# Recommender head on one Trainium2 core: the odd batch tiles enter the weight stream 57 units behind the even ones instead of 43

## The chip, the cores and the metric

The kernel runs on one core of a Trainium2 chip. The metric is device time in microseconds of one launch, the median of several executions. All data is fp32 in HBM at the start and the scores are in HBM at the end.

## What is computed

For 1024 samples. `x` is [1024, 50, 300], `label_embedding` is [1024, 200, 300]. Cut to what matters:

```python
def _attn_pool(x, mask, w_a, b_a, w_b):
    score = exp((x @ w_a + b_a) @ w_b)
    score = where(mask == 0, PAD, score)
    p = softmax(score, axis=1)
    return einsum('bne,bn->be', x, p[..., 0])
mask = sign(sum(abs(x), axis=2))[..., None]
q1 = _attn_pool(x, mask, w1, b1, w2)
q2 = _attn_pool(x, mask, w3, b3, w4)
h = concatenate([q1, q2], axis=1) @ w5 + b5          # [1024, 300]
f6 = h @ w6 + b6
iu, ju = triu_indices(300, k=1)                       # 44850 pairs
g = (v @ v.T)[iu, ju]
f7 = (h[:, iu] * h[:, ju] * g) @ w7 + b7              # w7 is [44850, 300]
out8 = concatenate([f6, f7], axis=1) @ w8 + b8
return einsum('bu,bku->bk', out8, label_embedding)    # [1024, 200]
```

The cost lies in three places: f7 (44850 products per sample, and a matmul over them), the two dot products of each of the 50 (padded to 56) rows of x, and the dot products with the 200 label rows of each sample.

## The kernel before

**Work and tiles.** The samples are cut into 8 batch tiles of 128 (b = 0 to 7), and for x into 16 half tiles of 64. The 44850 pairs are laid out as 351 tiles of 128 pairs, grouped by a table of 91 *units* (`UNITS`, `unit_table()`), most of them of four tiles. A unit names its left operand (A, B, C or a rotated copy such as A64, all parts of h transposed) and one of 25 buffers of rotated right operands. The first 57 units use the eight A buffers (seven units each, eight in the first), then come the B buffers (units 57 to 81), then six units of the rest, then three units ("own", units 88 to 90) whose two operands are both gathered in small pieces. The end of the table with these three is called a turn in what follows. VectorE multiplies left and right into `cring` (`products`, L917 for two batch tiles at once, L905 once per tile where only one is live; four slots), and TensorE multiplies them with the unit's part of w7 into the batch tile's accumulator (`unit`, L600, 128 x 300 fp32, which the trace shows as two MATMULs).

**The counter q.** Every engine walks through the same steps q, from START = -34 to STOP. Step q of 0 to POS - 1 does unit q of the stream, which is entry q mod 91 of the table. w7 is streamed over and over, in blocks of two units (1200 KB, `w7_load`, L729, from ScalarE's queue, three slots). Batch tile b takes part from BEGIN[b] to END[b] = BEGIN[b] + 91. Even tiles begin at 0, 91, 182, 273, odd ones SHIFT units later. While two are live, one block of w7 serves both. So SHIFT units at the head and SHIFT units at the end have one tile (*one-tile units*), all others two (*two-tile units*). In two-tile units ScalarE multiplies w7 by g (`w7_scale`, L738); in one-tile units VectorE folds g into its products. POS is the last END, 407 before.

**x and its dots.** Half tile s is read by the steps DOTS[s] = (first, past the last). In each of them VectorE makes the share of 56 dot rows (`score_row`, L819), ScalarE the sums of absolute values (`absolute`, L663). Maxima, softmax weights, pooling on TensorE (L549), turning and the product with w5 (`mix`, L563) follow at fixed distances (`LATE`): MIX is 12 steps behind the last dot step, and writes the left operands of tile b, in the buffers that tile b - 4 had.

**Labels.** Behind END[b] the tile's f7 is closed and out8 made. From LATER = 11 steps behind END[b], the 200 label rows of tile b are worked off, 150 KB each, loaded by fives (a *chunk* of 750 KB, `l_load`, L391, from SP's queue): VectorE makes one dot per row (`label_row`, L935). LABELS_BY says how many rows are done by the end of a step. For tile b they are spread over the steps up to END[b+1] + LATER, where a step that also has x dots counts one and another counts two. For tile 6, only EARLY_ROWS of its rows are done before POS. All other rows of tiles 6 and 7 come after POS, five a step, without any unit beside them: TAIL_CHUNKS chunks. Four in five of these are *shared*: VectorE makes the product of the chunk (L931), ScalarE the five row sums (`sums`, L747).

**Loads of h.** h is written to HBM (`hrows`) and read back in rotated form by SP's queue (`s_load`, L426 for the buffers, L433 to L446 for the three "own" units in many small pieces), for each live tile, three slots ahead. They stand in the same queue as x and labels, in the order of q.

**What the change and the steps of the prediction touch:** SHIFT (L140) and through it BEGIN, END, POS and BOTH; DOTS (L166); EARLY_ROWS (L205) and LABELS_BY; `products`, `unit`, `w7_scale`, `label_row`, `sums`.

Of the kernel before, what the change touches and what calls it, by code (L numbers as in the profile page):

```python
# [32 lines left out]
def unit_table():  # L33

    units, buf = [], 0
    for k in range(NA):
        first = 1 if k == 0 else 0
        units.append(("A", buf, first, QUAD - first))
        units.append(("B", buf, 0, QUAD))
        if k == 0:  # L40
            units.append(("A32", buf, 0, 1))
        units.append(("A64", buf, first, QUAD - first))
        for left in ("B32", "B64", "B96", "C"):
            units.append((left, buf, 0, QUAD))
        buf += 1
    for k in range(NB):
        first = 1 if k == 0 else 0
        units.append(("B", buf, first, QUAD - first))
        if k == 0:
            units.append(("B32", buf, 0, 1))  # L50
        units.append(("B64", buf, first, QUAD - first))
        units.append(("C", buf, 0, QUAD))
        buf += 1
    for k in range(ND):
        units.append(("A", buf, 0, QUAD))
        units.append(("B", buf, 0, QUAD))
        buf += 1
    for n in CUSTOM:
        units.append(("own", buf, 0, n))
        buf += 2  # L60
    return units, buf
# [37 lines left out]
UNITS, BUFS = unit_table()  # L99
# [7 lines left out]
def rec_kernel(nc, x, label, w13, w24, w5, w6t, w8, bcols, b8, w7p, vleft, vright, out):  # L107
# [29 lines left out]

    SHIFT = next(k for k, u in enumerate(UNITS) if u[1] == 6)  # L140
    BEGIN = [NU * (b // 2) + SHIFT * (b % 2) for b in range(NBT)]
    END = [p + NU for p in BEGIN]
    POS = END[-1]
    BOTH = END[-2] - SHIFT

# [4 lines left out]
    def live_at(n):  # L150
# [13 lines left out]


    DOTS = [(-34, -27), (-27, -20), (-20, -6), (-6, 6), (6, 24), (24, 43), (43, 54), (54, 65), (65, 77), (77, 89),  # L166
            (100, 114), (123, 137), (146, 160), (169, 183), (192, 206), (215, 229)]
    START = DOTS[0][0]
    ROWS = [(t // T, t % T, hd) for t in range(TT) for hd in range(2)]

# [31 lines left out]


    LATER = 11
    EARLY_ROWS = 65  # L205
    LABELS_BY = {START - 1: 0}
    for q in range(START, POS):
        done = 0
        for b in range(NBT - 1):
            steps = range(END[b] + LATER, END[b + 1] + LATER if b < NBT - 2 else POS)  # L210
            share = [1 if any(a <= k < z for a, z in DOTS) else 2 for k in steps]
            rows = K if b < NBT - 2 else EARLY_ROWS
            done += rows * sum(w for k, w in zip(steps, share) if k <= q) // sum(share)
# [30 lines left out]
    with ctx:  # L244
# [280 lines left out]
        def _(pe):  # L525
# [57 lines left out]
            def unit(p):  # L583
# [5 lines left out]
                pe.wait_ge(c_ready, p + 1)  # L589
                if SHIFT <= p < SHIFT + BOTH:  # L590
                    pe.wait_ge(w7_ready, p - SHIFT + 1)
                else:
# [50 lines left out]
        def _(act):  # L643
# [80 lines left out]
            def w7_load(n):  # L724
                k = BLOCKS[n][1]
                a, z = UNIT_TILE[k * WUNITS] * E, UNIT_TILE[min((k + 1) * WUNITS, NU)] * E
                if n >= WSLOTS:
                    act.wait_ge(c_used, LAST[n - WSLOTS] + 1)
                act.dma_start(wring[:, n % WSLOTS, 0:z - a], w7p[:, a:z]).then_inc(w7_in[n % WSLOTS], 16)  # L729

            def w7_scale(p):
                n, u = BLOCK_OF[p], p % NU
                first = UNIT_TILE[FROM[n] % NU]
                if p == max(FROM[n], SHIFT):
                    act.wait_ge(w7_in[n % WSLOTS], 16 * (n // WSLOTS + 1))
                for t in range(UNIT_TILE[u], UNIT_TILE[u + 1]):
                    w = wring[:, n % WSLOTS, (t - first) * E:(t - first + 1) * E]
                    ins = nc.scalar.activation(w, w, ACT.Copy, scale=gcol[:, t:t + 1])  # L738
                ins.then_inc(w7_ready, 1)
# [13 lines left out]
            for q in range(START, STOP):  # L753
# [7 lines left out]
                if 0 <= q < POS:  # L761
                    if q in FROM and FROM.index(q) + 2 < len(BLOCKS):
                        w7_load(FROM.index(q) + 2)
                    if SHIFT <= q + AHEAD < SHIFT + BOTH:
                        w7_scale(q + AHEAD)
# [241 lines left out]
```

## Time and profile before

| | us |
|---|---|
| median of 3 runs | 1860.07 |
| lowest, highest | 1859.95, 1860.88 |
| the profiled execution | 1859.29 |
| its span, first to last instruction | 1857.5 |
| TensorE busy | 1615.5 (87%) |
| VectorE busy | 1479.9 (80%) |
| ScalarE busy | 919.1 (49%) |
| moved by DMA | 617 MB, mean 332 GB/s |
| mean granted TensorE clock | 0.952 |

The engines overlap, so the busy times don't add up. A share is a mean over the head (x alone, then one-tile units), the long middle with two tiles, the one-tile units at the end and the labels behind them; each has its own limit, and what 14 units more or less are worth there is read from the stretch itself.

### The profile page before, as it was taken

The numbers are of one execution on the slowest core, as the hardware profiler recorded it, in microseconds if no ns is written. First come the engines' busy times: TensorE is split into PE (matmuls) and PEld (weight loads), VectorE is DVE, ScalarE is ACT, GpSimd is POOL, SyncE is SP. The second block draws the span as 40 slices with busy tenths as digits, with TensorE's granted clock in tenths as the row PEclk, the third lists the DMA queues.
The fourth block names the chain that finished last, engine by engine and source line by source line (L and its number), as shares of the span: only waits on it lengthen the run. The fifth ranks groups of instructions, "written<-read, shape, count | busy, mean of one in ns | idle before, by whom it ended". The sixth has DMA issues, their size and how long they took to land.

```text
span 1857.5 us, 25035 instructions
## 1 busy us (share of the span) xinstructions
PE 1615.5 (87%) x7142; PEld 1165.1 (63%) x7142; DVE 1479.9 (80%) x5516; ACT 919.1 (49%) x2844; POOL 33.4 (2%) x62
## 2 busy tenths in 40 slices
PE   0569999999999999997999999999999999998300
PEld 0236677776777767774777777767777777666200
DVE  8898986863699989967899976758777677498996
ACT  4433376654564636463465634434444444200698
POOL 0000000000000000000000000000000000000000
PEclk9889999999999999998999999999999999999655
DMA  7669867767789898998989999999999899899895
GB/s 279 237 256 352 344 245 260 264 222 278 263 301 420 324 401 335 389 334 308 381 300 407 352 394 386 364 294 403 355 342 342 305 385 354 272 420 421 338 417 244
DMA packets 139215, 617.00 MB, mean 332 GB/s; under 512 B 16432, under 2 KB 43693, under 8 KB 106181
## 3 DMA queue, kind: packets, MB, share of 16 engines
q1 hardware_dynamic: 105157, 368.23, 52.8%
q10 hardware_dynamic: 31744, 244.16, 34.0%
q0 software_dynamic: 2176, 3.01, 0.5%
q8 instruction: 57, 0.93, 0.2%
q14 instruction: 81, 0.66, 0.1%
HBM read 611.55 MB, written 3.79 MB: 331 GB/s over the span
## 4 chain that ended last, share of the span: by engine, by line
PE 72%; DMA 7%; ACT 7%; DVE 7%; SPq 4%; issue 2%; ACTq 0%; POOL 0%; DVEq 0%; POOLq 0%
PE bank L600 64%; ACT stream L747 6%; DMA wring<-in_w7p 5%; DVE junk L819 3%; PE bank L549 3%; SPq L438 3%; PE bank L563 2%; DMA sring<-hrows 2%; DVE stream L935 1%; PE bank L612 1%; PE bank L610 1%; DVE cring L917 1%; DVE cring L905 1%; ACT absjunk L663 1%; SPq L444 0%
## 5 line engine op out<-in xcount | busy, mean ns | idle before, releaser
L600 PE MATMUL bank<-wring,cring 128*128 128x300 f32 (+1 forms) x5616 | 1448.0, 419 | 52.8 <-DVE cring L917 19.6
L600 PEld LDWEIGHTS bank<-wring,cring 128*128 128x128 f32 (+1 forms) x5616 | 1064.1, 191 | 420.8 <-DVE cring L905 30.4
L738 ACT ACTIVATE wring<-wring,gcol 128x300 f32<-128x300 f32 x1237 | 565.1, 533 | 608.8 <-PE bank L600 340.3
L935 DVE SCALAR_TENSOR_TENSOR stream<-stream,out 128x300 f32<-128x300 f32 x1335 | 546.4, 466 | 0.9 <-DMA stream<-in_label 0.2
L917 DVE TENSOR_TENSOR cring<-lefts,sring 128x1024 f32<-128x1024 f32 (+2 forms) x309 | 368.3, 1193 | 205.1 <-PE bank L600 202.6
L819 DVE SCALAR_TENSOR_TENSOR junk<-stream,ubc 128x300 bf16<-128x300 f32 x896 | 364.2, 466 | 4.3 <-DMA stream<-in_x 4.2
L663 ACT ACTIVATE absjunk<-stream 128x300 bf16<-128x300 f32 x448 | 196.3, 440 | 50.3 <-PE bank L600 48.6
L747 ACT ACTIVATE stream<-stream 128x300 f32<-128x300 f32 x265 | 115.5, 441 | 0.1
L549 PE MATMUL bank<-stream,wts 128*32 128x300 f32 x896 | 66.6, 453 | 55.8 <-DVE small L861 55.8
L935 DVE DVE_READ_ACCUMULATOR stream<-stream,out 128x1 f32 x1335 | 109.9, 82 | 0.0
L905 DVE SCALAR_TENSOR_TENSOR cring<-lefts,gcol,sring 128x128 f32<-128x128 f32 x334 | 95.2, 348 | 16.8 <-PE bank L600 15.7
L931 DVE TENSOR_TENSOR stream<-stream,out 128x1500 f32<-128x1500 f32 x53 | 89.6, 1717 | 3.5 <-DMA stream<-in_label 1.8
L549 PEld LDWEIGHTS bank<-stream,wts 128*32 128x32 f32 x896 | 29.8, 118 | 90.8 <-issue 66.3
L663 ACT ACTIVATION_READ_ACCUMULATOR absjunk<-stream 128x1 f32 x448 | 84.6, 189 | 0.0
L819 DVE DVE_READ_ACCUMULATOR junk<-stream,ubc 128x1 f32 x896 | 74.0, 83 | 0.0
L917 DVE TENSOR_TENSOR cring<-sring 128x1024 f32<-128x1024 f32 (+1 forms) x12 | 11.5, 956 | 72.4 <-DMA sring<-hrows 49.1
L652 ACT ACTIVATE flat<-bank 128x300 f32<-128x300 f32 x8 | 3.2, 405 | 105.6 <-PE bank L600 105.6
L747 ACT ACTIVATION_READ_ACCUMULATOR stream<-stream 128x1 f32 x265 | 50.5, 190 | 0.0
L563 PE MATMUL bank<-poolT,w5sb 128*128 128x128 f32 (+3 forms) x288 | 48.2, 297 | 1.0 <-ACT poolT L652 0.8
L563 PEld LDWEIGHTS bank<-poolT,w5sb 128*128 128x128 f32 (+3 forms) x288 | 35.2, 164 | 14.4 <-issue 4.5
L838 DVE TENSOR_SCALAR masked<-absum 128x28 f32<-128x28 f32 x16 | 2.9, 178 | 38.6 <-ACT small L669 38.6
L655 ACT ACTIVATE lefts<-bank,bcol 128x128 f32<-128x128 f32 x16 | 5.9, 366 | 43.6 <-PE bank L563 42.7
(62 smaller groups left out, 247.7 us busy)
## 6 DMA issues: line engine op xcount, KB each, us to landing
stream<-in_label SPq DMA_DIRECT2D x320, 750.0 KB, 8.2
wring<-in_w7p ACTq DMA_DIRECT2D x184, 1200.0 KB, 8.4
stream<-in_x SPq DMA_DIRECT2D x64, 1050.0 KB, 12.6
sring<-hrows SPq DMA_DIRECT2D x152, 256.0 KB
wring<-in_w7p ACTq DMA_DIRECT2D x9, 1050.0 KB, 8.6
wring<-in_w7p ACTq DMA_DIRECT2D x9, 600.0 KB, 7.5
lefts<-hrows SPq DMA_DIRECT2D x48, 64.0 KB, 2.6
sring<-hrows SPq DMA_DIRECT2D x32, 88.0 KB
```

Source lines behind the costliest of these rows:

```text
L438: sp.dma_start(tiles[r0:r1, j0:j0 + ni, :], src).then_inc(s, 16)
L549: pe.matmul(dst[j * M:(j + 1) * M, 0:E], wts[:, j * T + t].rearrange("p h b -> p (h b)"), xring[:, X_SLOT[s * PARTS + j], t, :], start=(t ...
L563: mm = pe.matmul(dst[0:n, 0:P], w5sb[0:nk, q, o:o + n], poolT[0:nk, q % NCH, q // NCH, :], start=(q == 0), stop=(q == 2 * NCH - 1))
L600: mm = pe.matmul(acc[b % 4][:, 0:E], cring[0:rows, p % CSLOTS, b % 2, j0 + j, :], w, start=(p == BEGIN[b] and j == 0), stop=(p == END[b] - ...
L663: nc.scalar.activation(absjunk[:, k % 2, :], xring[:, X_SLOT[n], r % T, :], ACT.Abs, accum_out=absum[:, s % 3, r:r + 1]).then_inc(abs_done, 1)
L738: ins = nc.scalar.activation(w, w, ACT.Copy, scale=gcol[:, t:t + 1])
L747: ins = nc.scalar.activation(row, row, ACT.Copy, accum_out=score[:, m % 2, q0 + k:q0 + k + 1])
L819: ins = nc.vector.scalar_tensor_tensor(out=junk[:, k % 2, r % 2, :], in0=xring[:, X_SLOT[n], t, :], scalar=1.0, in1=ubc[:, hd, 0:E], op0=A ...
L905: ins = nc.vector.scalar_tensor_tensor(out=cring[0:rows, p % CSLOTS, b % 2, j, :], in0=one, scalar=gcol[0:rows, t:t + 1], in1=sring[0:rows ...
L917: nc.vector.tensor_tensor(cut(cring, p % CSLOTS), in0, cut(sring, nb % SSLOTS), ALU.mult).then_inc(c_ready, 1)
L931: nc.vector.tensor_tensor(rows, rows, out8[:, m % 4, :].unsqueeze(1).to_broadcast([P, LR, E]), ALU.mult).then_inc(l_product, 1)
L935: ins = nc.vector.scalar_tensor_tensor(out=row_in, in0=row_in, scalar=1.0, in1=out8[:, m % 4, :], op0=ALU.mult, op1=ALU.mult, accum_out=sc ...
```

## The change

SHIFT is now the first unit of buffer 8 (the first B buffer), 57, where it was the first unit of buffer 6, 43. Worked out from the table: odd tiles begin at 57, 148, 239, 330 (before 43, 134, 225, 316); POS is 421 for 407; the units with two tiles are 57 to 363, 307 for 321; w7 is read in 213 blocks for 206. The last six half tiles' dots are moved: the first of them by 3 steps, the others by 6. EARLY_ROWS is 95 for 65, so TAIL_CHUNKS is 61 for 67 and the shared chunks are 48 for 53. The intervals over which a tile's 200 label rows are spread, END[b] + 11 to END[b+1] + 11, are 57 and 34 steps long in turn, where they were 43 and 48.

```diff
-    SHIFT = next(k for k, u in enumerate(UNITS) if u[1] == 6)
+    SHIFT = next(k for k, u in enumerate(UNITS) if u[1] == 8)
...
     DOTS = [(-34, -27), (-27, -20), (-20, -6), (-6, 6), (6, 24), (24, 43), (43, 54), (54, 65), (65, 77), (77, 89),
-            (100, 114), (123, 137), (146, 160), (169, 183), (192, 206), (215, 229)]
+            (103, 117), (129, 143), (152, 166), (175, 189), (198, 212), (221, 235)]
...
-    EARLY_ROWS = 65
+    EARLY_ROWS = 95
```

What it does to VectorE's order at three places. Names: `cring` holds the products for TensorE, `junk` takes the x dots, `stream` is the ring of x and label rows.

VectorE at unit 43 and behind it, before:

```order
L905 SCALAR_TENSOR_TENSOR cring<-lefts,gcol,sring 128x128 x4
L819 SCALAR_TENSOR_TENSOR junk,small<-stream,ubc 128x300 x3
L917 TENSOR_TENSOR cring<-lefts,sring 128x1024
L819 SCALAR_TENSOR_TENSOR junk,small<-stream,ubc 128x300 x5
L838 TENSOR_SCALAR masked<-absum 128x28
```

The same place now:

```order
L905 SCALAR_TENSOR_TENSOR cring<-lefts,gcol,sring 128x128 x4
L819 SCALAR_TENSOR_TENSOR junk,small<-stream,ubc 128x300 x3
L905 SCALAR_TENSOR_TENSOR cring<-lefts,gcol,sring 128x128 x4
L819 SCALAR_TENSOR_TENSOR junk,small<-stream,ubc 128x300 x5
L838 TENSOR_SCALAR masked<-absum 128x28
```

The dot rows stay where they were; the product beside them is that of one tile in four instructions, for units 43 to 56.

VectorE at units 178 and 179 (the last before the "own" units, and the first of these), before:

```order
L917 TENSOR_TENSOR cring<-lefts,sring 128x1024
L819 SCALAR_TENSOR_TENSOR junk,small<-stream,ubc 128x300 x4
L935 SCALAR_TENSOR_TENSOR stream,score<-stream,out 128x300 x3
L917 TENSOR_TENSOR cring<-sring 128x1024
L819 SCALAR_TENSOR_TENSOR junk,small<-stream,ubc 128x300 x4
```

Now:

```order
L917 TENSOR_TENSOR cring<-lefts,sring 128x1024
L819 SCALAR_TENSOR_TENSOR junk,small<-stream,ubc 128x300 x4
L935 SCALAR_TENSOR_TENSOR stream,score<-stream,out 128x300 x4
L917 TENSOR_TENSOR cring<-sring 128x1024
L819 SCALAR_TENSOR_TENSOR junk,small<-stream,ubc 128x300 x4
```

There are four to five label rows a step beside four dot rows, for three before; in the steps of this interval without dots there are eight or nine.

VectorE at the end of the units (L931 is the first shared chunk), before:

```order
L905 SCALAR_TENSOR_TENSOR cring<-lefts,gcol,sring 128x128 x4
L935 SCALAR_TENSOR_TENSOR stream,score<-stream,out 128x300 x2
L905 SCALAR_TENSOR_TENSOR cring<-lefts,gcol,sring 128x128 x4
L935 SCALAR_TENSOR_TENSOR stream,score<-stream,out 128x300 x3
L931 TENSOR_TENSOR stream<-stream,out 128x1500
```

Now:

```order
L905 SCALAR_TENSOR_TENSOR cring<-lefts,gcol,sring 128x128 x4
L935 SCALAR_TENSOR_TENSOR stream,score<-stream,out 128x300 x2
L905 SCALAR_TENSOR_TENSOR cring<-lefts,gcol,sring 128x128 x4
L935 SCALAR_TENSOR_TENSOR stream,score<-stream,out 128x300 x8
L931 TENSOR_TENSOR stream<-stream,out 128x1500 x4
```

The one-tile units with some two label rows each run for 14 units more, and the labels behind them begin with one chunk that isn't shared.

## Rows read from the trace of the kernel before

**Rows 1.** the page's slices, TensorE, busy tenths of 40 equal slices
```profile
PE   0569999999999999997999999999999999998300
```

**Rows 2.** stretches: start:end us, length, then each engine's busy us (instructions), PEclk, DMA share, GB/s
```profile
105.80:172.20 66.40, 54.29 (x269) 36.95 (x270) 60.44 (x284) 20.10 (x84) 3.52 (x6) 1.00 0.81 322
172.20:220.30 48.10, 43.39 (x220) 30.58 (x219) 45.41 (x210) 14.68 (x62) 0.00 (x0) 1.00 0.93 363
220.30:280.70 60.40, 60.40 (x296) 44.32 (x295) 50.42 (x198) 41.95 (x135) 0.00 (x0) 1.00 0.66 245
280.70:482.80 202.10, 199.07 (x999) 142.67 (x998) 123.08 (x435) 117.61 (x361) 7.04 (x12) 0.99 0.72 262
482.80:733.70 250.90, 250.90 (x1117) 184.97 (x1116) 228.39 (x900) 140.77 (x405) 7.59 (x13) 1.00 0.90 343
733.70:896.10 162.40, 148.52 (x662) 106.25 (x661) 130.98 (x518) 76.48 (x213) 0.00 (x0) 0.95 0.94 349
896.10:1147.50 251.40, 251.25 (x1120) 185.19 (x1119) 215.48 (x832) 132.74 (x365) 8.15 (x14) 1.00 0.95 368
1147.50:1285.00 137.50, 134.82 (x531) 99.53 (x530) 94.36 (x319) 58.87 (x133) 0.58 (x1) 1.00 0.96 352
1285.00:1515.30 230.30, 230.30 (x911) 171.94 (x910) 169.21 (x574) 103.00 (x231) 0.58 (x2) 1.00 0.94 344
1515.30:1622.20 106.90, 103.25 (x403) 77.04 (x402) 64.79 (x214) 40.81 (x91) 0.00 (x0) 0.98 0.94 324
1622.20:1650.50 28.30, 25.18 (x94) 16.45 (x94) 28.30 (x134) 1.71 (x5) 0.00 (x0) 1.00 1.01 412
1650.50:1680.80 30.30, 27.14 (x103) 18.58 (x102) 27.86 (x123) 0.00 (x0) 0.54 (x1) 1.00 1.01 419
1680.80:1720.20 39.40, 35.24 (x136) 24.82 (x134) 31.85 (x133) 0.00 (x0) 0.00 (x0) 1.00 1.01 422
1720.20:1857.50 137.30, 16.02 (x43) 8.51 (x41) 117.75 (x199) 117.15 (x535) 1.08 (x2) 0.54 0.82 332
```

**Rows 3.** the same columns for instructions on cring alone (PE, PEld, DVE), units 284 to 340
```profile
1285.00:1515.30 230.30, 225.70 (x894) 169.35 (x893) 68.54 (x58) 1.00 0.94 344
```

**Rows 4.** waits, 1640 to 1730 us: waiter <- awaited, total us, times, longest
```profile
PE bank L600 <- DMA wring<-in_w7p: 8.6, 13, 1.7
```

**Rows 5.** DMA issues, 1640 to 1730 us: count, KB each, median us to landing
```profile
wring<-in_w7p ACTq DMA_DIRECT2D x17, 1200.0 KB, 9.8
stream<-in_label SPq DMA_DIRECT2D x17, 750.0 KB, 27.4
```

**Rows 6.** groups by line, ScalarE from 1728 us: busy us, mean ns, idle before
```profile
L747 ACT ACTIVATE stream<-stream 128x300 f32<-128x300 f32 x265 | 115.5, 441 | 0.1
```

**Rows 7.** timeline of VectorE, 218 to 222 us: start us, us, instruction
```profile
218.12 1.14 DVE L905 SCALAR_TENSOR_TENSOR cring<-lefts,gcol,sring 128x128 f32<-128x128 f32 x4
219.18 0.46 DVE L819 SCALAR_TENSOR_TENSOR junk<-stream,ubc 128x300 bf16<-128x300 f32 x1
...
220.35 1.22 DVE L917 TENSOR_TENSOR cring<-lefts,sring 128x1024 f32<-128x1024 f32 x1
221.49 0.47 DVE L819 SCALAR_TENSOR_TENSOR junk<-stream,ubc 128x300 bf16<-128x300 f32 x1
```

**Rows 8.** waits, 790 to 880 us, the turn of units 179 to 181
```profile
DVE cring L917 <- issue: 12.1, 2, 10.1
...
DVE cring L917 <- DMA sring<-hrows: 9.4, 1, 9.4
```

**Rows 9.** stretches as in rows 2: two turns, and units 375 to 406
```profile
1220.00:1250.00 30.00, 28.52 (x114) 21.17 (x113) 12.17 (x40) 10.36 (x24) 0.00 (x0) 1.00 0.91 288
1590.00:1620.00 30.00, 26.34 (x99) 19.42 (x98) 9.52 (x33) 7.74 (x17) 0.00 (x0) 0.94 0.86 253
1650.50:1720.20 69.70, 62.39 (x237) 43.40 (x235) 59.71 (x255) 0.00 (x0) 0.54 (x1) 1.00 1.01 421
```

**Rows 10.** waits of the loading queue SP, 1150 to 1290 us
```profile
SPq L391 <- DVE stream L935: 58.7, 19, 4.1
```

## The prediction

> **What bounds the kernel now.** I read four views, in this order, and tied each to the counter that orders the program, the unit number (0 to 406). The slices of the page come first [rows 1]: TensorE stands at nine tenths nearly all the way from the fifth slice to the thirty-seventh. The last two have no TensorE work and belong to the labels. To see where a unit lies in time, the stretches [rows 2] are cut at unit starts, which the products themselves show: in the stretches of product work alone [rows 3], 2 x 57 batch-tile units give 58 VectorE instructions and 894 matmul instructions. That stretch (units 284 to 340) took 230.3 us, 4.04 us a unit, with TensorE busy throughout and its clock at full speed. A unit of two batch tiles is 16 matmul instructions of 225.70/894 = 0.2525 us, which is those 4.04 us; a unit of one tile is 8 of them, **2.02 us at TensorE's pace**.
>
> Three kinds of time follow. With two tiles live (units 43 to 363, 220.3 to 1622.2 us) TensorE sets the pace: it is busy 60.4 of 60.4, 199.1 of 202.1, 230.3 of 230.3 us, and loses only in the stretches around the turns of the unit table (units 88 to 90, 179 to 181, ...), 13.9 us in units 159 to 192. With one tile live a unit does not run at 2.02 us: units 24 to 42 took 48.1 us, 2.53 each, with VectorE busy 45.4 us of it; units 390 to 406 took 39.4 us, **2.32 each**, with the transfers at 422 GB/s [rows 2]. There TensorE waits 13 times, shortly, for the w7 block [rows 4]; a block takes 9.8 us to land and a label chunk 27.4 us [rows 5]. After the last unit the labels have 137.3 us to themselves, ScalarE busy for 117.2 of it [rows 2], nearly all in row sums: 265 of them, 115.5 us [rows 6].
>
> By the starts of VectorE's instructions [rows 7], the four products of a one-tile unit take 1.06 us (218.12 to 219.18), three dot rows 1.17, so 0.39 each (to 220.35), the product of a two-tile unit 1.14 (to 221.49). Label rows have the same shape and I give them the same 0.39.
>
> **The change, part by part.** Total matmul work is the same. Fourteen units that had two tiles become twenty-eight with one: 14 at the head (43 to 56) and 14 behind the old end (407 to 420). The w7 stream is read for 421 units in place of 407, seven more blocks of 1200 KB [rows 5], 8.6 MB. ScalarE scales w7 for 14 units less; it is busy 103.0 us of 230.3, so that hides and is worth nothing.
>
> Head, units 43 to 101. It took 60.4 + 202.1 = 262.5 us. It loses 14 x 4 matmuls of two instructions, 112 x 0.2525 = 28.3 us. But the x dots of tile 3 have not moved, so VectorE keeps its 50.4 busy us, less 14 x 0.08. By the ratio of busy time to span in the two one-tile stretches before it (60.4 of 66.4, 45.4 of 48.1) 49.3 us of work take 52 to 54 us; I take 53. TensorE's own part there is 60.4 + about 11 of work that it carried over (its lag of up to four units) - 28.3 = 43 us, so 10 us of idle time come in. 262.5 - 28.3 + 10 = 244.2: **-18.3 us** (-21 to -14).
>
> The label rate. Tile b's 200 rows are spread evenly from END[b]+11 to END[b+1]+11. These intervals were 43 and 48 units long and are now 57 and 34. In the three short ones the rate is 5.9 rows a unit for 4.2. In the long ones (units 102 to 158, 193 to 249, 284 to 340) TensorE was busy 250.9 of 250.9, 251.3 of 251.4 and 230.3 of 230.3 us already, and fewer rows bring nothing: **0**.
>
> Units 159 to 192. Label rows go from 156 to 200, and because the dots were moved later, the dot rows from 64 to 84. 64 rows x 0.39 = 25.1 us on a VectorE that was busy 131.0 of 162.4, so 156.1. It also stood idle for the small loads of the turn, 9.4 and 12.1 us [rows 8], which more rows do not shorten, since they are in its own order behind the products: 156.1 + 21.5 = 177.6, **+15.2** (0 if the idle time takes them up, +25 if none does).
>
> Units 250 to 283. 58 more label rows of 150 KB are 8.9 MB; 137.5 us at 352 GB/s were 48.4 MB, now 57.3. In the 30 us of the turn the queues moved only 288 GB/s [rows 9], 8.6 MB. The other 48.7 MB at the 421 GB/s held in units 375 to 406 take 115.7 us; 145.7 us in all, **+8.2**. TensorE's 134.8 and VectorE's 94.4 + 22.7 = 117.1 lie under it. Units 341 to 374: 106.9 at 324 and 28.3 at 412 GB/s are 46.3 MB, plus 8.9 is 55.2; the turn took 7.6 MB in 30 us (253 GB/s), the rest 113.1 us: 143.1 for 135.2, **+7.9**. Ends for each: 0, and +26 if the bytes move at the stretch's old mean (57.3/0.352 = 163; 55.2/0.342 = 161).
>
> Here the Trainium skill speaks against 421 GB/s: its page "DMA: Bandwidth & Descriptors", section "Where 436 GB/s comes from", says that for HBM to SBUF the HBM side binds, at about 358 GB/s. The trace disagrees, since 421 were held for 69.7 us [rows 9]; by the rule the two stretches would take 160 and 154 us and the sum be 26 us higher.
>
> Units 375 to 406: 66 label rows for 65, the same 31 or 32 units: 0. Units 407 to 420: fourteen at the 2.32 us of the seventeen before them, **+32.5**; ends 28.3 (TensorE's 2.02) and 35.4 (the 2.53 of units 24 to 42).
>
> The label tail. 30 more rows of tile 6 are done beside the units (95 for 65), so 61 chunks stay for 67, and 48 shared chunks for 53. Five times five row sums of 115.5/265 = 0.436 us: **-10.9**. By the mean of a chunk (137.3/67) it would be -12.3; if VectorE or a load took over, down to -8. ScalarE stays the bound: 61 chunks are 47 MB, 111 us at 421, with up to 13 in the ring before the tail.
>
> Sum: -18.3 + 15.2 + 8.2 + 7.9 + 32.5 - 10.9 = +34.6. The profiled execution took 1859.29 (span 1857.5), 0.8 below the median of the three runs, 1860.07: **1894 us**, slower by 1.8%.
>
> **Rivals.** *The dense stretches cost nothing.* VectorE's idle time and the rings take up the burst of labels: -18.3 + 32.5 - 10.9 = +3.3, 1863 us. For it: VectorE had 31 idle us in units 159 to 192 and 43 in 250 to 283. Against: two thirds of the first is the wait at a turn. Chance 0.10, on both sides of the 0.2% (3.7 us) that a measurement of this kernel can tell from no change.
>
> *One-tile units at TensorE's pace,* the one on the other side. If dots and w7 loads keep up with 2.02 us, the head loses all of its 28.3 us, the tail adds 28.3 and the labels give back 10.9: 1848 us, if the dense stretches cost nothing. With the head at my 53 us it decides from 2.09 us a unit at the tail downwards: 14 x 2.09 = 29.2 = 18.3 + 10.9. For it: units 375 to 389 took 30.3 us, 2.02 each [rows 2]. Against: the seventeen behind them did not, at the same row rate, and at the head VectorE alone has 49.3 us of work where TensorE's pace asks for 43. Chance 0.04.
>
> *The queues don't hold 421 GB/s in a mixed stretch.* Units 250 to 283 and 341 to 374 carry w7, labels and many small loads, and reached 352 and 342 GB/s without being short of requests. If these are their limits, those two cost 25 and 26 us in place of 8 and 8, and the tail units 35.4: 1894 + 17 + 18 + 3 = 1932 us. For it: the transfers' busy share was 0.96 already at 352 GB/s [rows 2]. Against: the queue that issues the label loads waited 58.7 us, 19 times, for VectorE to free a slot [rows 10], so the rate was what was asked for. The 358 of the skill's page named above would mean this case. Chance 0.18.
>
> **How the numbers follow.** Forecast 0.68, for 1894 us; its own bounds (the dense stretches between 10 and 50 together, the tail 28.3 to 35.4) reach from 1868 to 1915. I leave out the fast rival, most of the one at 1863 and what of the slow one lies beyond its price: **1866 to 1934**. Faster by over 0.2%: 0.04. Within: 0.05, from the case at 1863. Slower: 0.91.
>
> **What would show it right or wrong.** In the changed profile: the first two-tile product (L917) should stand at 273 us for 220.3; units 43 to 56 should show VectorE over 0.9 busy and TensorE near 0.8. Unit 102 should begin near 464.5 for 482.8. Units 159 to 192 should take about 178 us with VectorE at 156. The stretches 250 to 283 and 341 to 374 should take some 145 us at over 380 GB/s, with waits for label or w7 loads on the path. From the last two-tile unit to the end of units should be 57 one-tile units in 138 us for 43 in 98. ScalarE's row sums should be 240, and the part behind the last unit 126 us. The forecast is wrong if the head takes over 60 us (VectorE's rows are slower beside one-tile products), if unit 364 begins within 10 us of where the head leaves it (no cost of dense labels), or if the last fourteen units run at 2.1 us.

## The result, and the profile after

The changed kernel takes **1917.72 us**, the median of 4 runs (1914.53 to 1922.06), against 1860.01 for the kernel before on the same chip (4 runs, 1859.52 to 1860.88): ratio 1.0311, 95% interval 1.0289 to 1.0333. It is slower by 57.7 us. The forecast was 1894 us, slower, with a range of 1866 to 1934. The profiled execution is the longest of the four, 1922.06 us with a span of 1920.3, so the trace below explains 62.8 us.

The stretches of the changed kernel, cut at the same unit starts as [rows 2] and with the same columns (length, busy us of PE, PEld, DVE, ACT, POOL, PEclk, DMA share, GB/s). In order: units 43 to 56, 57 to 101, 102 to 158, 159 to 192, 193 to 249, 250 to 283, 284 to 340, 341 to 363, 364 to 374, 375 to 406, 407 to 420, and the rest:

```profile
219.40:269.00 49.60, 44.74 (x234) 30.25 (x233) 48.86 (x240) 21.30 (x90) 2.37 (x5) 1.00 0.81 300
269.00:461.00 192.00, 188.22 (x948) 134.84 (x947) 119.67 (x419) 114.02 (x351) 4.65 (x8) 0.99 0.74 275
461.00:723.80 262.80, 257.16 (x1117) 187.75 (x1116) 206.89 (x780) 136.34 (x381) 7.13 (x13) 0.97 0.82 305
723.80:908.00 184.20, 157.88 (x693) 111.92 (x691) 154.43 (x640) 88.14 (x251) 0.48 (x1) 0.94 0.91 335
908.00:1145.30 237.30, 237.30 (x1053) 175.03 (x1054) 195.35 (x728) 124.40 (x346) 4.00 (x7) 1.00 0.87 338
1145.30:1312.30 167.00, 149.42 (x566) 107.39 (x565) 117.09 (x434) 60.55 (x136) 4.24 (x8) 0.93 0.96 363
1312.30:1542.60 230.30, 230.30 (x911) 171.91 (x910) 146.56 (x457) 103.55 (x232) 0.97 (x2) 1.00 0.86 312
1542.60:1656.80 114.20, 104.14 (x401) 77.39 (x399) 80.17 (x294) 40.09 (x89) 0.00 (x0) 0.94 0.96 348
1656.80:1692.50 35.70, 29.15 (x100) 18.27 (x99) 35.70 (x172) 1.71 (x5) 0.00 (x0) 0.95 1.01 413
1692.50:1765.30 72.80, 64.63 (x246) 45.56 (x246) 60.54 (x263) 0.00 (x0) 0.54 (x1) 1.00 1.01 420
1765.30:1794.20 28.90, 25.67 (x98) 17.98 (x98) 25.40 (x109) 0.00 (x0) 0.00 (x0) 1.00 1.01 421
1794.20:1920.30 126.10, 16.19 (x45) 8.53 (x43) 107.02 (x184) 106.27 (x485) 1.08 (x2) 0.55 0.81 329
```

Against [rows 2] the difference, stretch by stretch:

| units | before | forecast of the change | after | change |
|---|---|---|---|---|
| 43 to 101 | 262.5 | -18.3 | 241.6 | -20.9 |
| 102 to 158 | 250.9 | 0 | 262.8 | +11.9 |
| 159 to 192 | 162.4 | +15.2 | 184.2 | +21.8 |
| 193 to 249 | 251.4 | 0 | 237.3 | -14.1 |
| 250 to 283 | 137.5 | +8.2 | 167.0 | **+29.5** |
| 284 to 340 | 230.3 | 0 | 230.3 | 0.0 |
| 341 to 374 | 135.2 | +7.9 | 149.9 | +14.7 |
| 375 to 406 | 69.7 | 0 | 72.8 | +3.1 |
| 407 to 420 | none | +32.5 | 28.9 | +28.9 |
| behind the units | 137.3 | -10.9 | 126.1 | -11.2 |

Head, the fourteen units behind the old end, and the label tail came out within 4 us of their terms. The largest part that was not forecast lies in units 250 to 283, around the turn at units 271 and 272. Ten microseconds at a time, there:

```profile
1230.00:1240.00 10.00, 10.00 (x42) 7.50 (x41) 1.69 (x10) 4.69 (x11) 0.00 (x0) 1.00 1.02 357
1240.00:1250.00 10.00, 6.21 (x25) 4.42 (x24) 3.32 (x12) 3.04 (x7) 0.00 (x0) 1.00 1.02 281
1250.00:1260.00 10.00, 2.27 (x9) 1.35 (x8) 0.26 (x2) 1.42 (x3) 0.00 (x0) 0.81 0.75 204
1260.00:1270.00 10.00, 5.78 (x12) 3.94 (x13) 4.72 (x19) 0.00 (x0) 0.00 (x0) 0.50 0.43 132
1270.00:1280.00 10.00, 9.79 (x38) 6.51 (x37) 10.00 (x44) 2.77 (x7) 0.00 (x0) 1.00 0.94 349
1280.00:1290.00 10.00, 8.38 (x28) 5.14 (x27) 10.00 (x40) 6.39 (x16) 0.00 (x0) 0.85 1.01 426
1290.00:1300.00 10.00, 10.00 (x25) 5.78 (x25) 7.78 (x32) 3.34 (x8) 0.00 (x0) 0.64 1.01 412
1300.00:1310.00 10.00, 10.00 (x41) 7.55 (x40) 8.85 (x30) 3.60 (x8) 0.00 (x0) 1.00 1.02 415
```

TensorE is busy 6.21, then 2.27 of 10 us, and the clock that it is granted falls to 0.81 and 0.50, which is 1.2 of 2.4 GHz; it comes back (1.00) and falls once more (0.85, then 0.64). In 1290 to 1300 us TensorE is busy all ten microseconds and gets through 25 matmul instructions, where it does 41 at full clock in the next ten. Before, the clock stayed at 1.00 over the whole of this stretch [rows 2]. While TensorE waits the transfers move only 281, 204 and 132 GB/s. In the first of these rows the DMA engines were nevertheless busy all the time (share 1.02, with which they moved 426 GB/s in 1280 to 1290 us); only in the next two, at 0.75 and 0.43, had they time to spare. What VectorE waited for, first after, then before:

```profile
DVE cring L917 <- issue: 15.0, 2, 12.7
DVE cring L917 <- DMA sring<-hrows: 15.0, 1, 15.0
```

```profile
DVE cring L917 <- DMA sring<-hrows: 10.4, 1, 10.4
DVE cring L917 <- issue: 4.7, 1, 4.7
```

30.0 us for the turn's gathers, where it was 15.1. (The "issue" waits stand before products of the same gathered operands, whose smallest DMAs the view gives no landing for, so I count them with the gathers.) From the product of unit 269 to that of unit 272 VectorE took 40.7 us, for 25.1 before; the same measure, three products of a turn, is used for the other kernels below. And the queue that issues them, with start and length:

```profile
1239.60 1.31 SPq L391 DMA_DIRECT2D stream<-in_label  x2
1241.07 9.76 SPq L438 DMA_DIRECT2D sring<-hrows  x6
1250.88 0.57 SPq L391 DMA_DIRECT2D stream<-in_label  x1
1251.62 4.54 SPq L438 DMA_DIRECT2D sring<-hrows  x6
```

Label chunks (L391) stand between the gathers (L438), and six gathers then take 9.76 us merely to be issued.

Units 102 to 158, forecast at zero, are a second such part, +11.9 us. TensorE did 1117 instructions there before and after, but now stood idle for 5.6 us of it, and its clock of 0.91 from 650.9 us on made its work 6.3 us longer:

```profile
650.90:723.80 72.90, 67.26 (x303) 46.07 (x302) 47.48 (x183) 27.98 (x77) 3.62 (x7) 0.91 0.82 317
```

```profile
690.70 1.36 PE L608 MATMUL bank<-brow,ones 1*128 1x300 f32 x2 [4.20 <-ACT poolT L652]
```

L608 begins out8 of tile 1, and stood behind ScalarE's copy of the turned pooled sums of half tile 11 (`poolT`). In the changed kernel both fall in step 151; before, they fell in steps 137 and 145. All five kernels of this document with SHIFT at 57 took 262.2 to 262.8 us in these units, with a wait of 4.2 to 4.8 us at this instruction and a mean clock of 0.97; all nine with 43, f1 with the moved dots among them, took 250.8 to 252.0 without that wait. So the shift of the tiles brings it; that the meeting in one step is the reason is argued from the trace and not shown, since no run separates the two in the changed kernel.

### The profile page after: what moved, and what is told of

The parts are those of the page before. It is cut to its first block, busy times and chain, and to the rows that moved or that the text cites. A ratio compares the mean times of both kernels' runs of the same rounds, so it can differ in the third digit from the quotient of the medians.

```text
span 1920.3 us, 25109 instructions
## 1 busy us (share of the span) xinstructions
PE 1638.1 (85%) x7142; PEld 1171.6 (61%) x7142; DVE 1495.1 (78%) x5659; ACT 884.3 (46%) x2738; POOL 33.2 (2%) x62
## 4 chain that ended last, share of the span: by engine, by line
PE 63%; DVE 14%; DMA 8%; ACT 7%; SPq 5%; issue 3%; ACTq 0%; POOL 0%; DVEq 0%; POOLq 0%
PE bank L600 55%; DMA wring<-in_w7p 5%; ACT stream L747 5%; DVE junk L819 5%; DVE stream L935 4%; SPq L438 3%; PE bank L563 2%; PE bank L549 2%; DMA sring<-hrows 2%; DVE cring L917 2%; DVE cring L905 2%; PE bank L612 1%; PE bank L610 1%; SPq L433 1%; ACT absjunk L663 1%
## 5 line engine op out<-in xcount | busy, mean ns | idle before, releaser
L600 PE MATMUL bank<-wring,cring 128*128 128x300 f32 x5616 | 1463.4, 421 | 98.3 <-DVE cring L917 52.2
L600 PEld LDWEIGHTS bank<-wring,cring 128*128 128x128 f32 x5616 | 1067.8, 192 | 478.9 <-DVE cring L917 61.8
L738 ACT ACTIVATE wring<-wring,gcol 128x300 f32<-128x300 f32 x1181 | 538.6, 532 | 620.2 <-PE bank L600 358.1
L935 DVE SCALAR_TENSOR_TENSOR stream<-stream,out 128x300 f32<-128x300 f32 x1360 | 556.7, 465 | 1.2 <-DMA stream<-in_label 0.7
L917 DVE TENSOR_TENSOR cring<-lefts,sring 128x1024 f32<-128x1024 f32 (+2 forms) x295 | 351.3, 1192 | 230.3 <-PE bank L600 227.1
L905 DVE SCALAR_TENSOR_TENSOR cring<-lefts,gcol,sring 128x128 f32<-128x128 f32 x446 | 126.6, 344 | 22.0 <-PE bank L600 14.8
L747 ACT ACTIVATE stream<-stream 128x300 f32<-128x300 f32 x240 | 104.6, 452 | 0.1
L917 DVE TENSOR_TENSOR cring<-sring 128x1024 f32<-128x1024 f32 (+1 forms) x12 | 11.5, 956 | 95.7 <-issue 59.8
L549 PEld LDWEIGHTS bank<-stream,wts 128*32 128x32 f32 x896 | 29.8, 118 | 90.1 <-issue 65.6
L931 DVE TENSOR_TENSOR stream<-stream,out 128x1500 f32<-128x1500 f32 x48 | 80.9, 1716 | 1.7 <-DMA stream<-in_label 0.2
L563 PE MATMUL bank<-poolT,w5sb 128*128 128x128 f32 (+3 forms) x288 | 48.1, 297 | 0.8 <-ACT poolT L652 0.8
L563 PEld LDWEIGHTS bank<-poolT,w5sb 128*128 128x128 f32 (+3 forms) x288 | 35.2, 165 | 14.2 <-issue 4.5
```

What stands on the lines that cost most here:

```text
L549: pe.matmul(dst[j * M:(j + 1) * M, 0:E], wts[:, j * T + t].rearrange("p h b -> p (h b)"), xring[:, X_SLOT[s * PARTS + j], t, :], start=(t ...
L563: mm = pe.matmul(dst[0:n, 0:P], w5sb[0:nk, q, o:o + n], poolT[0:nk, q % NCH, q // NCH, :], start=(q == 0), stop=(q == 2 * NCH - 1))
L600: mm = pe.matmul(acc[b % 4][:, 0:E], cring[0:rows, p % CSLOTS, b % 2, j0 + j, :], w, start=(p == BEGIN[b] and j == 0), stop=(p == END[b] - ...
L747: ins = nc.scalar.activation(row, row, ACT.Copy, accum_out=score[:, m % 2, q0 + k:q0 + k + 1])
L905: ins = nc.vector.scalar_tensor_tensor(out=cring[0:rows, p % CSLOTS, b % 2, j, :], in0=one, scalar=gcol[0:rows, t:t + 1], in1=sring[0:rows ...
L917: nc.vector.tensor_tensor(cut(cring, p % CSLOTS), in0, cut(sring, nb % SSLOTS), ALU.mult).then_inc(c_ready, 1)
```

## The experiments

**Theory A**: the label rate is what costs. The intervals of 57 and 34 steps in place of 43 and 48 make bursts of 5.9 rows a unit, all three of them over a turn. More label chunks are then freed, and so asked for, just where the gathers go through the same queue, and the gathers come late. **Rivals**: the offset of the tiles, or the later dots, with which TensorE's side work falls elsewhere (B); or the one-tile units themselves, by their queues or their own pace (E). Three sets of four kernels; in these the kernel before ran at 1863.63, 1860.98 and 1860.35 us (its single runs between 1852.88 and 1869.01), so differences under some 4 us are not told apart by medians.

**e1, the bursts alone, on the kernel before.** Used as `range(EDGES[b], EDGES[b + 1])` in the loop that fills LABELS_BY:

```diff
+    EDGES = (102, 159, 193, 250, 284, 341, 375, POS)
```

> The kernel before (odd tiles at 43, its own dots and EARLY_ROWS) with the label rows of the changed kernel's intervals: 200 rows between steps 102, 159, 193, 250, 284, 341 and 375. Theory A (the bursts of labels at 5.9 rows a unit cost the time, above all at the turns): units 102 to 374 take 50 to 64 us longer than before, as in the changed kernel, so 1910 to 1924 us. Rival B (the shifted tiles or the moved dots cost it): within 8 us of 1860. Rival C (more bytes than the queues carry, a matter of both): half, about 1885.

Measured 1903.05 us against 1863.63, ratio 1.0203 (1.0164 to 1.0243). Units 159 to 192, 193 to 249, 250 to 283 and 341 to 374:

```profile
736.80:914.90 178.10, 157.52 (x687) 112.78 (x686) 146.97 (x603) 79.41 (x220) 0.60 (x1) 0.93 0.95 357
914.90:1159.60 244.70, 244.70 (x1094) 180.28 (x1093) 194.47 (x717) 130.39 (x361) 8.04 (x14) 1.00 0.87 328
1159.60:1318.50 158.90, 141.54 (x539) 103.06 (x538) 116.65 (x435) 59.70 (x135) 0.07 (x1) 0.96 0.95 364
1546.80:1695.50 148.70, 134.65 (x491) 95.84 (x489) 115.75 (x461) 41.86 (x95) 0.00 (x0) 0.92 0.98 366
```

Units 102 to 374 took 1209.5 us for 1167.7, 41.8 more; the changed kernel took 1231.5, 63.8 more. So the bursts alone, with every tile, dot and one-tile unit where it was, bring two thirds of what was added to these stretches in the changed kernel. Of the other 22 us, 12.0 lie in units 102 to 158, which took 250.8 us here. The time lies below theory A's band (1910 to 1924), above rival C's 1885 and far above rival B's 8 us: A holds for most, not for all.

**e2, the changed kernel with the bursts of tiles 1 to 4 evened out.**

```diff
+    EDGES = (102, 159, 204, 250, 295, 341, 375, POS)
```

> The changed kernel with the label rows of tiles 1 to 4 spread evenly (intervals from 159 on: 45, 46, 45, 46 steps, 4.4 rows a unit); the last short interval, 341 to 375, stays. Theory A: units 159 to 192 fall from 184 to about 163 us, 250 to 283 from 167 to about 138, units 193 to 249 rise from 237 to about 250: 1880 to 1886 us. Rival B (shifted tiles, moved dots): 1912 to 1922.

1900.75 us (ratio to before 1.0191, 1.0156 to 1.0227), 17 less than the changed kernel (20.6, if each is held against the kernel before of its own set) and 15 short of theory A. Units 159 to 192 fell to 169.7 and 250 to 283 to 152.9, two thirds and half of the way back. An even rate of 4.4 rows does not restore the turns.

**e3, even, and no label rows at the turns.**

```diff
-            share = [1 if any(a <= k < z for a, z in DOTS) else 2 for k in steps]
+            share = [0 if k % NU >= 82 else 1 if any(a <= k < z for a, z in DOTS) else 2 for k in steps]
```

> As the even one, and no label rows in the nine steps up to and with each turn (q mod 91 of 82 to 90), the others of the interval somewhat denser. Theory A with its mechanism (a chunk of labels that is freed in the turn is loaded ahead of the turn's small loads in the same queue, and these come late): the waits at the turns shrink, another 10 to 20 us less than the even one, 1862 to 1872. Rival D (the small loads are slow by themselves, the labels only a matter of VectorE's and the queues' total): no less than the even one, 1880 to 1890.

1877.56 us (1.0083, 1.0050 to 1.0116), another 23 less, though 6 above theory A's band. Units 159 to 192 took 160.7 and 250 to 283 took 141.9; from unit 269 to unit 272 it was 23.3 us for e2's 32.8. The total number of rows and bytes is that of e2; only nine steps of each 91 are spared. Rival D, which had no less than the even kernel's time, is out.

**e4, the same on the kernel before**, which turns the reason into a gain:

```diff
-            share = [1 if any(a <= k < z for a, z in DOTS) else 2 for k in steps]
+            share = [0 if k % NU >= 82 else 1 if any(a <= k < z for a, z in DOTS) else 2 for k in steps]
```

> The kernel before with no label rows in the nine steps of each turn. TensorE lost 13.9 us in units 159 to 192, 2.7 in 250 to 283 and 3.7 in 341 to 363. Theory A with its mechanism: most of it comes back, 1843 to 1852 us. Rival D: 1858 to 1865, the waits at the turns as before.

**1841.42 us** (1841.40 to 1843.47), ratio 0.9882 (0.9849 to 0.9915): faster than both kernels, by 22 us against the median of before in its set, and a little more than theory A had expected. Units 159 to 192, 250 to 283 and 341 to 363:

```profile
731.60:887.70 156.10, 147.40 (x660) 105.63 (x659) 127.18 (x505) 74.34 (x207) 0.00 (x0) 0.97 0.92 347
1138.70:1274.50 135.80, 134.78 (x531) 99.53 (x530) 89.39 (x292) 57.66 (x130) 0.17 (x1) 1.00 0.92 352
1504.80:1599.60 94.80, 94.80 (x377) 71.36 (x376) 55.57 (x168) 40.57 (x91) 0.00 (x0) 1.00 0.88 335
```

The last, the third turn, took 94.8 us for 106.9, with TensorE busy in all of it. The span is 17.9 us shorter than that of before: -6.3, -1.7 and -12.1 in these three stretches, +4.7 in units 364 to 374, and small amounts elsewhere. The last two belong together, since TensorE does part of the third turn's work behind unit 364 now: units 341 to 374 took 127.8 us for 135.2, 7.4 less. The expectation had added up 20.3 us of lost TensorE time; the sum came near, but not by its parts: the turn of units 179 to 181, the first with label rows, was to give 13.9 us and gave 6.3. From unit 269 to 272 and from 360 to 363 VectorE took 16.7 us each, for 25.1 and 28.3 before.

**f1, only the dots moved, on the kernel before.**

```diff
-            (100, 114), (123, 137), (146, 160), (169, 183), (192, 206), (215, 229)]
+            (103, 117), (129, 143), (152, 166), (175, 189), (198, 212), (221, 235)]
```

> The kernel before with only the dots moved as in the change (the last six half tiles 3 and 6 steps later). Theory A (bursts of labels and the turns): the dots are of no account, 1856 to 1868 us. Rival B2 (the moved dots, which now begin 7 steps before the turn of units 179 to 181, cost it): units 159 to 192 at least 5 us longer than the 162.4 of before, and 1870 or more.

1862.58 us (1.0011, 0.9992 to 1.0030): no difference. Inside, the trace has units 159 to 192 in 166.4 us for 162.4 (rival B2 asked for 5 more), 193 to 249 in 241.7 for 251.4 and 250 to 283 in 150.0 for 137.5. The pooling and mixing of the last half tiles fall some steps later. 33 of the mixing's matmul instructions (L563), which had stood in units 193 to 249, come behind the start of unit 250, here and in the changed kernel: some 5.5 us, since 36 of them took 6.00 us there. The rest of the 12.5 us is 3.6 us more idle time of TensorE and a clock of 0.98. So of the 29.5 us in 250 to 283 some 5.5 are a shift and not a loss, with their counterpart in 193 to 249, which the forecast had at zero.

**f2, the changed kernel with EARLY_ROWS at 65.**

```diff
-    EARLY_ROWS = 95
+    EARLY_ROWS = 65
```

> The changed kernel with EARLY_ROWS back at 65: 30 label rows (4.6 MB) go from beside the last one-tile units to the label tail, which gets 10 to 11 us longer. Theory A with the queues as the bound of the one-tile units (421 GB/s): the 4.6 MB less make units 375 to 420 some 11 us shorter, 102 to 91, and the whole is the same, 1914 to 1922 us. Rival E (these units run at their own pace of w7 latency and TensorE): they stay at 102 us, and the whole is 1926 to 1930.

1920.59 us (1.0329, 1.0284 to 1.0374), not to be told from the changed kernel's 1.0311. Units 375 to 420, and the rest:

```profile
1682.30:1782.30 100.00, 90.09 (x343) 63.73 (x343) 76.44 (x313) 0.00 (x0) 0.54 (x1) 1.00 1.00 407
1782.30:1918.60 136.30, 16.12 (x44) 8.78 (x42) 117.31 (x197) 117.16 (x535) 1.08 (x2) 0.54 0.79 319
```

Thirty rows less made the 46 units 1.7 us shorter (100.0 for 101.7), while the tail grew by the expected 10.2 us. So these units were not bound by the sum of the bytes, as theory A had it: between 1.4 and 2.1 label rows each they take some 2.2 us whatever the labels do. Rival E had this right, but its 1926 to 1930 us for the whole did not come. The whole doesn't show the 8 us that follow, because the stretches ahead were some 10 us shorter in this execution, for no reason of the edit; the total decides nothing here, the stretch does.

**f3, even to the end, and turns free.**

```diff
+    EDGES = (102, 159, 204, 250, 295, 341, 386, POS)
```

> The changed kernel with all label intervals from tile 1 on even (the last from 341 to 386) and the turns free of label rows: nothing of the bursts is left. Theory A: units 341 to 374 fall from 151.7 to about 135, units 375 to 420 rise by the few rows that come there, 1862 to 1870 us. What stands then against the turn-free kernel before (1841) is the cost of the fourteen pairs of one-tile units themselves, +20 to +28; by the sum of head, tail and labels in the prediction it was +3. Rival: 1875 or more.

1881.92 us (1.0119, 1.0072 to 1.0166): no better than e3. Units 341 to 374 gave 22.7 us back (129.0 for e3's 151.7), and units 375 to 420 took nearly all of it. First f3, then e3:

```profile
1635.70:1761.90 126.20, 101.72 (x362) 69.34 (x361) 109.03 (x495) 0.00 (x0) 0.54 (x1) 0.95 1.01 420
```

```profile
1644.30:1749.90 105.60, 93.27 (x342) 65.72 (x343) 87.71 (x371) 0.00 (x0) 0.54 (x1) 0.97 1.01 419
```

By the schedule, 157 label rows stand beside these units in f3 and 95 in e3: 62 rows for 20.6 us, 0.33 us each, with the queues at 420 GB/s. Beyond about two rows a unit, a label row beside a one-tile unit costs about what it costs in the tail (f2: 10.2 us for thirty, 0.34 each). The expected 1862 to 1870 fell with that.

**f4, label rows kept, their loads moved behind the turn's gathers, to step 88.**

```diff
         free = L_END[L_BEFORE[n]] if L_BEFORE[n] is not None else X_WIDE_DONE if n < NARROW else X_DONE
+        if 82 <= free % NU < 88:
+            free += 88 - free % NU
```

> The kernel before with the label rows in their places, but every load of a label chunk that falls in steps 82 to 87 of a turn issued at step 88, behind the turn's gathers. Theory A's mechanism in its strict form (the labels' bytes stand ahead of the gathers in the same queue): most of the gain of the turn-free kernel, 1843 to 1852 us. Rival F (it is VectorE's rows in the turn, or the bytes of w7 on the other queue): 1858 to 1868 us.

1862.26 us (1.0007, 0.9985 to 1.0028): no gain, and by its number in rival F's band. (The profiled execution is the longest of nine, 1872.37 us.) But the waits moved with the loads, for which rival F gives no reason. (Lines stand two further down in this kernel and the next: L919 is L917, L393 is L391, L440 is L438, L446 is L444.) VectorE's products of units 179, 180 and 181 (start, length, idle time before), and the queue:

```profile
833.83 1.23 DVE L919 TENSOR_TENSOR cring<-sring 128x1024 f32<-128x1024 f32 x1 [3.43 <-issue]
...
839.75 1.23 DVE L919 TENSOR_TENSOR cring<-sring 128x1024 f32<-128x1024 f32 x1 [1.95 <-issue]
...
856.33 0.42 DVE L919 TENSOR_TENSOR cring<-sring 50x256 f32<-50x256 f32 x1 [12.61 <-issue]
```

```profile
841.00 1.78 SPq L393 DMA_DIRECT2D stream<-in_label  x4
842.95 1.97 SPq L446 DMA_DIRECT2D sring<-hrows  x4
```

The first two products, which had come 13.4 and 14.0 us behind the one before them, now came after 7.4 and 5.9; the third, whose gathers (L446) were still to be issued when four label chunks went out at step 88, came after 16.6 in place of 6.0. It was the same at the two later turns, 18.3 and 18.4 us ahead of the third product.

**g1, the same, but behind all gathers, for the wide ring.**

```diff
         free = L_END[L_BEFORE[n]] if L_BEFORE[n] is not None else X_WIDE_DONE if n < NARROW else X_DONE
+        if n >= L_WIDE and free % NU >= 82:
+            free += NU - free % NU
```

> The kernel before with its label rows in place; for the chunks of the wide ring (thirteen slots, from tile 3 on) a load that falls in steps 82 to 90 of a turn is issued in the first step behind it, behind all of the turn's gathers. In the earlier deferral (to step 88) four chunks stood in the midst of the gathers, and the wait moved to the last of them. Theory A's mechanism (bytes ahead of the gathers in their own queue): the two late turns (units 271 and 272, 362 and 363) take some 7 us each as in the turn-free kernel, in place of 13 and 8, 17 and 6; 250 to 283 falls by 3 to 6, 341 to 363 by 8 to 12, the first turn stays: 1843 to 1852 us. Rival F: 1858 or more.

1862.50 us (1.0011, 0.9984 to 1.0038): again no gain, and in rival F's band. At the two later turns the waits nevertheless went as theory A has it. From unit 269 to 272 VectorE took 16.8 us for 25.1, from 360 to 363 16.5 for 28.3, as little as in e4, while its label rows and the w7 loads stayed in their steps; its busy time in units 341 to 363 is the 64.79 us of before. So it is the loads of labels that delay the gathers, and rival F is out. The queue at the second turn, with the last twelve of fifteen gathers issued in 6.43 us (all fifteen in 10.66), where the changed kernel needed 9.76 for six and 4.54 for the next six:

```profile
1224.48 6.43 SPq L440 DMA_DIRECT2D sring<-hrows  x12
1231.07 1.28 SPq L446 DMA_DIRECT2D sring<-hrows  x4
```

and units 341 to 363, with the third turn, then units 375 to 406:

```profile
1514.00:1609.20 95.20, 95.20 (x378) 71.63 (x377) 64.79 (x214) 40.96 (x92) 0.00 (x0) 1.00 0.85 304
...
1640.40:1724.30 83.90, 66.66 (x246) 46.48 (x246) 59.17 (x255) 0.00 (x0) 0.54 (x1) 0.96 1.01 421
```

95.2 us for 106.9, as in e4 (126.4 for 135.2 over units 341 to 374). Units 250 to 283 took 137.3 us for 137.5, where 3 to 6 us less were expected: TensorE had stood idle for only 2.7 us there before, so that shorter waits of VectorE were worth nothing. But the labels' bytes that had not moved during the turn had to move later: units 375 to 406 took 83.9 us for 69.7, at 421 GB/s, and gave all of it back. In e4 the rows themselves, and with them their loads, are done ahead of the turn, beside two-tile units.

One question is left open by all of these. e4 and g1 take the label bytes out of the turn altogether, so they don't tell whether the gathers came late because they stood behind the chunks in their queue, or because both need the same DMA engines, which were fully busy in 1240 to 1250 us of the changed kernel. No run issued the labels from another queue.

**g2 and g3, the width of the free window**, 80 and 85 for 82:

```diff
-            share = [0 if k % NU >= 82 else 1 if any(a <= k < z for a, z in DOTS) else 2 for k in steps]
+            share = [0 if k % NU >= 80 else 1 if any(a <= k < z for a, z in DOTS) else 2 for k in steps]
```

> The turn-free kernel before, with eleven free steps (80 to 90) for nine. If chunks asked for just ahead of step 82 still delay the gathers, 3 to 6 us less than 1841; if the denser rows elsewhere decide, 1841 to 1848.

> The turn-free kernel before, with six free steps (85 to 90). Theory A: some of the waits at the first gathers come back, 1846 to 1854; the rival, that the rest of the burst matters more: 1836 to 1841.

1840.66 us (0.9884, 0.9859 to 0.9908) and 1848.88 us (0.9927, 0.9905 to 0.9950). Eleven free steps are as good as nine; with six, part of the waits returns: from unit 269 to 272 VectorE took 22.3 us (16.6 with eleven, 16.7 with nine), from 360 to 363 21.0 us (16.9 and 16.7). The stretch of units 250 to 283 decides less here, with 143.3 us for six, 141.1 for eleven and 135.8 for nine: in the two longer ones the granted clock was 0.95 and 0.96 in place of 1.00, with TensorE idle for less than 2 us in all three.

**g4, free turns and an earlier start of each tile's labels.**

```diff
-    LATER = 11
+    LATER = 8
```

> The turn-free kernel before, with the label rows begun 8 steps behind a tile's end in place of 11, so that 15 more rows (1158 for 1143) are done before the last two-tile unit. Theory G (a label row beside two-tile units is free, and one behind them costs some 0.36 us, beside one-tile units or in the tail): 5 us less than 1841, 1834 to 1838. Rival: the rows come out even, 1840 to 1843, or the earlier start waits for out8, over 1843.

1845.68 us (0.9910, 0.9890 to 0.9929). The profiled execution spans 1841.3 us for e4's 1839.6. Theory G's 5 us did not come: what units 364 to 374 gained (28.8 us for 33.0) units 375 to 406 lost (74.2 for 70.3), and units 250 to 283 took 5 us more, as they did in g2 without this edit. So that a row beside two-tile units is free, and saves its price elsewhere, was not confirmed; why units 375 to 406, with 60 rows for 65, took longer stays open. The median lies above the rival's 1840 to 1843. Waits for out8 are not the reason: VectorE's idle time ahead of all of its label rows adds up to 1.0 us.

## Why the prediction was right, and where it was off

**The sign and the balance of the ends.** Slower by 34.6 was forecast, 57.7 measured, inside the range. But 1917.72 lies above the forecast's own bounds (1868 to 1915); that the range still holds it is luck, since its upper part had been added for another case, queues that don't hold 421 GB/s. "Head, units 43 to 101: -18.3" gave -20.9 in the trace, with VectorE busy 48.9 of 49.6 us in units 43 to 56 (forecast 49.3 of 53): it runs fuller than in the one-tile stretches from which the ratio was taken. "Units 407 to 420: +32.5" gave 28.9, 2.06 us each; but with units 375 to 406 at 72.8 for an unchanged 69.7 the 46 units together took 101.7 us for a forecast 102.2. By the prediction's own sign ("if the last fourteen units run at 2.1 us") this term was wrong; its 2.32 us held as a mean alone: units 390 to 406 took 43.1 us, 2.5 each, and units 390 to 420 together 72.0, which is 2.32. "The label tail: -10.9" gave -11.2, with 240 row sums as forecast:

```profile
L747 ACT ACTIVATE stream<-stream 128x300 f32<-128x300 f32 x240 | 104.6, 452 | 0.1
```

**Dense labels, units 159 to 192: +15.2** gave +21.8 (e1: +15.7 by the bursts alone). VectorE's busy time is 154.4 us (forecast 156.1), but its idle time was 29.8 us where the forecast had kept 21.5. Some 8 of the 21.8 us are no loss: TensorE did 543 product instructions here for 512, and 859 for 892 in units 193 to 249, at 0.2525 us each. With the 5.5 us of mixing that moved behind unit 250 this makes up the -14.1 there.

**Units 250 to 283: +8.2** is the step that failed in size, +29.5. It read: "In the 30 us of the turn the queues moved only 288 GB/s", and kept those 30 us as they were while the label rate around them rose by 40%. The wait at the turn doubled (15.1 to 30.0 us), since label chunks are loaded among the gathers; e3, e4 and the turns of f4 and g1 show that it is these loads. The fall of TensorE's clock that goes with such a wait had no term at all. The 29.5 us come apart into 14.9 us more idle time of TensorE (17.6 for 2.7), some 5.5 us of mixing moved in from the stretch before, and some 9 us by which its slower clock (0.93 for 1.00) stretched the rest. The two signs named for this stretch, over 380 GB/s and waits for label or w7 loads on the path, did not come: it moved 363 GB/s, and the waits were for the gathers.

**Units 102 to 158: 0** is the other step that failed, +11.9. The forecast looked at the label rows alone there, and fewer of them did bring nothing; what it had no term for is TensorE's wait of 4.2 us ahead of out8 of tile 1, and the clock that fell with it. That -14.1 in units 193 to 249 nearly cancels it is chance: the one is a cost, the other work moved to its neighbours.

**The structure without bursts.** The prediction's rival "the dense stretches cost nothing" put the rest of the change at +3.3 us. Between e3 and e4, both with free turns, it is 34.9 us of span. Of these, 10.6 lie in units 102 to 158 and 23.9 in units 341 to 374: tile 5 ends 14 units later, its labels cannot start before step 341, 71 label rows fewer are done by then (1000 for 1071), and they have to go beside the one-tile units, where the queues are full, or into a burst. Head, units 407 to 420 and tail are -20.1, +34.4 and -12.1, near the forecast's terms. The term "units 341 to 374: +7.9" was therefore too small as well, and the changed kernel's +14.7 hides that, because the kernel before lost 7.4 us there to its own turn (135.2 against e4's 127.8).

**The rivals.** One-tile units at TensorE's pace: units 407 to 420 came near (2.06 us), the head did not. Queues that don't hold 421 GB/s: units 250 to 283 moved 363 GB/s and 341 to 363 moved 348, which looks like that case; its price for the two stretches was 25 and 26 us, and they took 29.5 and 14.7 more. The ten-microsecond rows speak for it in part. Behind the turn the transfers did move 426 and 412 GB/s; but in the turn the DMA engines were busy all the time at 357 and then 281 GB/s, so bytes among the gathers cost them more time, and over the whole stretch they were busy for 0.96 of it. Idle DMA engines (0.75 and 0.43 of two rows) account for some 8 us of 167. The changed stretch was thus short of spare DMA time too, which the forecast's 421 GB/s for all but 30 us had left out. The 358 GB/s of the Trainium skill (page "DMA: Bandwidth & Descriptors", section "Where 436 GB/s comes from") is again exceeded by the trace, 421 GB/s over units 407 to 420.

## What to carry to other kernels

When bulk loads and small gathers share a queue and its DMA engines, the rate of the bulk *at the moment of the gathers* counts, as e2 and e3 show, and not only its mean: keep the consumer that frees the bulk's slots still for those steps, and do its work ahead. A load that is only postponed comes back later, and here it came back where the queues were already full. And when work is moved along a schedule, ask which rows can no longer be done beside the slow, two-tile units: their cost appears far from the edit. Ask also which rare pieces of work now fall in one step: where two met in step 151, 12 us came with them.

## What was unexpected of the hardware

The time to issue the same small gather varies widely. Six behind two label chunks took 9.76 us, or 1.6 each, in the changed kernel, and the next six, behind one, 4.54; with no chunk among them fifteen took 10.66 us at g1's second turn and 14.64 at f4's first, 0.7 and 1.0 each. What sets it the runs don't show. And a wait costs TensorE more than the wait: it stood idle for 11.96 us, the granted clock went to 0.50, and it stayed there for some six microseconds after TensorE had begun to work again at 1264 us. It fell to 0.64 once more 30 us later, with 25 matmul instructions in ten microseconds where 41 are usual.
